# Narrow relation one-hots, two loads moved to ScalarE, and a check moved on GpSimd, in a one-core graph network kernel

## The reference

```
h = relu(layernorm(x))
for W_r, W_sl, W_el in two layers:
    msg = (rel_embed[edge_type] + h[src]) @ W_r
    agg = segment_sum(msg, dst)
    h = rrelu(agg * norm + where(in_degree == 0, h @ W_el, h @ W_sl))
x = x + h
# then one layer of graph attention over the same edges, and x + its output
```

## Time and profile before

| | |
|---|---|
| time, median of 3 runs | 776.05 us (775.11 to 777.04) |
| time of the profiled execution | 776.97 us |
| its span | 775.2 us |
| PE busy | 718.0 us (93%) |
| PE weight loads busy | 534.4 us (69%) |
| DVE busy | 513.9 us (66%) |
| ACT busy | 432.8 us (56%) |
| POOL busy | 279.3 us (36%) |

### The profile page before, as it was taken

The page is one execution under the profiler, slowest core; times in us unless marked ns, Lnnn a source line. Parts: engine busy times, 40 slices in busy tenths (PEclk is TensorE's granted clock), DMA queues, the critical chain, the costliest instruction groups (busy, mean ns, idle before and its releaser), DMA issues.

```text
span 775.2 us, 15480 instructions
## 1 busy us (share of the span) xinstructions
PE 718.0 (93%) x5805; PEld 534.4 (69%) x5805; DVE 513.9 (66%) x906; ACT 432.8 (56%) x1096; POOL 279.3 (36%) x293
## 2 busy tenths in 40 slices
PE   4686789999999999999999999799999999999996
PEld 2565788999899999889889998244444444444456
DVE  5999999988888877333234334245675757576676
ACT  1577566666666666641211223377676767767663
POOL 7299200000001222100000000366675757666664
PEclk9999999999999999999999999799999999999998
DMA  4101000133300000102231112110000100000010
GB/s 132 50 24 45 18 2 9 50 105 65 106 24 8 9 8 9 67 20 81 85 99 39 36 35 61 63 30 0 4 24 1 27 1 14 13 15 13 2 26 21
DMA packets 39763, 27.89 MB, mean 36 GB/s; under 512 B 5311, under 2 KB 38288, under 8 KB 39686
## 3 DMA queue, kind: packets, MB, share of 16 engines
q1 hardware_dynamic: 38514, 25.89, 11.5%
q10 hardware_dynamic: 1172, 0.98, 0.4%
HBM read 13.28 MB, written 10.80 MB: 31 GB/s over the span
## 4 chain that ended last, share of the span: by engine, by line
PE 71%; DMA 8%; DVE 8%; issue 5%; ACT 5%; SPq 2%; ACTq 1%; POOL 1%; POOLq 0%; DVEq 0%
PE sums L1568 17%; PE sums L1551 16%; PE sums L1047 12%; PE sums L1122 9%; PE sums L1086 8%; DVE work L876 3%; DMA x_after_messages<-work 2%; DMA h_attention<-work 2%; DMA work<-in_x 2%; SPq L580 2%; PE sums L1054 1%; DMA counts<-in_x 1%; DVE work L870 1%; ACT counts L1335 1%; PE sums L1061 1%
## 5 line engine op out<-in xcount | busy, mean ns | idle before, releaser
L1647 POOL TENSOR_TENSOR counts<-counts,work 125x500 f32<-125x500 f32 x150 | 165.0, 1100 | 100.0 <-DVE work L1717 94.7
L1717 DVE SCALAR_TENSOR_TENSOR work<-sums,counts 125x500 f32<-125x500 f32 x150 | 101.5, 677 | 106.1 <-ACT sums L1671 100.7
L1086 PE MATMUL sums<-work 125*128 125x196 f16 (+15 forms) x1220 | 153.7, 253 | 17.9 <-DVE work L876 17.9
L1568 PE MATMUL sums<-work 125*128 125x500 f32 (+1 forms) x350 | 159.7, 546 | 6.8 <-DVE work L1717 6.2
L1551 PE MATMUL sums<-work 128*125 128x500 f32 x300 | 152.2, 589 | 0.0
L1666 ACT ACTIVATE sums<-sums,steady 125x500 f32<-125x500 f32 (+1 forms) x157 | 102.0, 650 | 75.0 <-PE sums L1551 71.8
L1335 ACT CAST counts<-sums 128x364 f32 (+38 forms) x305 | 131.6, 473 | 2.3 <-issue 1.1
L870 DVE TENSOR_TENSOR work<-work,counts 125x3024 f16<-125x3024 f16 (+1 forms) x60 | 114.4, 1906 | 25.9 <-PE sums L1088 25.3
L1088 PE MATMUL sums<-work 125*128 125x10 f16 (+15 forms) x800 | 131.5, 194 | 0.0
L876 DVE TENSOR_TENSOR work<-work,counts 125x4200 f16<-125x4200 f16 (+15 forms) x120 | 126.6, 1093 | 0.0
L1047 PE MATMUL sums<-counts 125*128 125x250 f16 (+1 forms) x975 | 119.6, 266 | 3.7 <-ACT work L1263 3.5
(11 more groups left out here) (184 smaller groups left out, 734.8 us busy)
## 6 DMA issues: line engine op xcount, KB each, us to landing
first_columns<-counts SPq DMA_DIRECT2D x5, 610.4 KB
counts<-first_columns SPq DMA_DIRECT2D x5, 610.4 KB
counts<-counts SPq DMA_DIRECT2D x5, 468.8 KB
counts<-in_x SPq DMA_DIRECT2D x5, 312.5 KB
h_nodes<-counts SPq DMA_DIRECT2D x5, 312.5 KB
work<-in_x SPq DMA_DIRECT2D x12, 125.0 KB
x_after_messages<-work SPq DMA_DIRECT2D x12, 125.0 KB
h_attention<-work SPq DMA_DIRECT2D x12, 125.0 KB
```

What stands on the lines that cost most here:

```text
L1086: pe.matmul(win[:, 0:c, cols], lo[:, k * 2 * LO:k * 2 * LO + 128], m[:, k, h0 * w:(h0 + c) * w].rearrange("p (h d) -> p h d", d=w), start= ...
L1568: last = pe.matmul(ps_o[c % 2][:, 0:cols(u) // n], h3[:, source(c, j + i), :], pbuf[u % PB][:, i * NP:i * NP + cols(u) // n], start=j + i ...
L1647: pool.tensor_tensor(a, a, p, ALU.add).then_inc(acc_done, 1)
L1717: dve.scalar_tensor_tensor(pbuf[u % PB], ps_s[u % 4][0:NP, 0:WIDE], float(np.exp(-CLIP)), counts[0:NP, source(c, j), target(c) * WIDE:(tar ...
```

## The change

Relations' one-hots get 100 columns and lie behind all the sources' one-hots of a batch, so that L870 becomes two instructions; the weight load of the relations takes exactly these 100 columns, and the matmul writes 100 partitions. ScalarE issues the loads of the last two pieces of x, after its first small copy. GpSimd waits for `words_done` ahead of its check and no longer behind it.

```diff
-    lo = view(work, at, NP, tiles * 2 * LO + 2, F16)
-    at += tiles * 2 * LO * 2
+    lo = view(work, at, NP, tiles * (LO + RL) + 2, F16)
+    at += tiles * (LO + RL) * 2
...
-            for i in range(5):
+            for i in range(3):
                 sp.dma_start(xs[:, 5 * i:5 * i + 5, :], ...).then_inc(x_in, 16)
...
-            pool.wait_ge(edges_in[0], 16)
+            pool.wait_ge(words_done, 1)
             pool.tensor_copy(final, dst_i[:, EDGES - 1:]).then_inc(outside_set, 1)
             pool.tensor_tensor(steps_i[:, 1:], dst_i[:, :-1], dst_i[:, 1:], ALU.subtract).then_inc(outside_set, 1)
...
             link(pool.memset(most[:, RT + 5:], 0.0))
-
-            pool.wait_ge(words_done, 1)
             pool.wait_ge(outside_set, 5)
...
-                dve.tensor_tensor(lo[:, 0:t * 2 * LO].rearrange("p (t c two) -> p t c two", c=LO // 2, two=2),
-                                  iota_h[:, None, 0:LO].rearrange("p o (c two) -> p o c two", two=2).broadcast_to([NP, 2 * t, LO // 2, 2]),
-                                  key_lo.rearrange("p t (k two) -> p (t k) two", two=2)[:, :, None, :].broadcast_to([NP, 2 * t, LO // 2, 2]), ALU.is_equal)
+                for k, c0, c in ((0, 0, LO), (1, t * LO, RL)):
+                    dve.tensor_tensor(lo[:, c0:c0 + t * c].rearrange("p (t c two) -> p t c two", c=c // 2, two=2),
+                                      iota_h[:, None, 0:c].rearrange("p o (c two) -> p o c two", two=2).broadcast_to([NP, t, c // 2, 2]),
+                                      key_lo[:, :, None, 2 * k:2 * k + 2].broadcast_to([NP, t, c // 2, 2]), ALU.is_equal)
...
-                            pe.matmul(win[:, 0:c, cols], lo[:, k * 2 * LO:k * 2 * LO + 128],
+                            pe.matmul(win[:, 0:c, cols], lo[:, k * LO:k * LO + 128],
                                       m[:, k, h0 * w:(h0 + c) * w]..., start=t == 0, stop=False, skip_group_check=True)
-                        last = pe.matmul(win[:, c:, cols], lo[:, (2 * k + 1) * LO:(2 * k + 1) * LO + 128],
+                        last = pe.matmul(win[0:RL, c:, cols], lo[:, n * GT * LO + k * RL:n * GT * LO + (k + 1) * RL],
                                          r[:, k, :]..., start=False, stop=False, skip_group_check=True)
...
             act.copy(woken, zeros[0:1, 0:1]).then_inc(first_keys, 1)
+            for i in range(3, 5):
+                act.dma_start(xs[:, 5 * i:5 * i + 5, :], ...).then_inc(x_in, 16)
```

More of the change, by code:

```diff
@@ L1230, in _ @@
             act.copy(woken, zeros[0:1, 0:1]).then_inc(first_keys, 1)
+            for i in range(3, 5):
+                act.dma_start(xs[:, 5 * i:5 * i + 5, :], x.rearrange("(j p) f -> p j f", p=NP)[:, 5 * i:5 * i + 5, :]).then_inc(x_in, 16)
             for i, k in enumerate(KEY_ORDER):
```

## The result

The changed kernel takes 772.76 us (median of 12 runs, 769.87 to 773.69), the kernel before beside it on the same chip 775.0 (12 runs). The ratio is 0.9967, with a 95% interval from 0.9955 to 0.998: 2.6 us faster by the ratio, 2.2 us by the medians. The same kernel, measured again on another chip, gave 0.9961 [0.9946, 0.9976], 3.0 us. The forecast was 773.8, or 2.25 us faster than 776.05. The difference is what was met. The time itself, 772.76, lies at what the rival "x early" gave (772.8), but x wasn't early: the kernel before took 1.05 us less beside the changed one than in the three runs on which the forecast was built. The profiled execution took 773.57 us (span 771.8), 3.4 us less than that of before.

The account below looks back on a forecast made before the run. VectorE bounds the path to 115.69 us, but for four places, then PE through the counting. One-hots -2.3, weight loads 0, PE's stretch at 91 us +0.1, head 0 give -2.2 us: 776.05 to 773.8 us, range 771.8 to 778.3.

Parts of the forecast that it names:

- x early: Rival at the head: x lands early, giving 1.1 us more, 3.3 in all, 772.8 us; chance 0.15.
- VectorE's saving: One-hots at L870: 0.147 us saved per four-group batch where VectorE is on the path, 2.3 us in all.
- nothing for batches 8 and 9: One-hots of batches 8 and 9: no gain, since VectorE then waits for the store of h_nodes.
- The narrow load: Relations' weight load at L1088: 100 columns take 46 ns, hidden behind the matmul ahead, cost 0.
- The rival with 9 us: L1088's loads, 130 to 322 us: 86 ns each, not hidden, 9 us cost, 782.8 us; narrow load bare, chance 0.17.
- a price per load: L1088: if a narrow load costs 57 ns whatever its width, 0.8 us is bare in the tiles of w = 10 and 11.
- The head: Loads of x and GpSimd's check, ahead of the statistics: gain 0, covered by the wait for x.
- 2.0 was the step: Batch 0's L870 or L876: collision with GpSimd's moved check costs VectorE 2.0 us, between 1.3 and 2.64.
- the mark of 12.74: ACT's first key copy: later than 12.74 us would show the forecast wrong.
- the signs of a bare load: PE from 130 to 322 us: a stretch over 1 us longer than 192 us would show the forecast wrong.
- Savings swallowed: Rival: store of h_nodes, PE's stretches and ACT's chain leave 0.9 us gain or less, 775.2 us; chance 0.18.
- What lies behind 322 us: Code after the counting: starts earlier by as much as was gained, since none of it waits for anything outside.

Follow-up runs that it names:

- e2: The kernel before with the last two x pieces loaded from ACT, nothing else changed; 776.45 us, ratio 1.0016.
- e3: The kernel before with GpSimd's check moved behind words_done, nothing else changed; 775.82 us, ratio 1.0004.
- e5: The kernel before with only the relations' weight loads narrowed to 100 columns, one-hots still 126 wide; 775.47 us, ratio 1.0005.
- r_e4: The changed kernel with the relations' weights loaded as 128 columns again, repeated on another chip; 772.38 us, ratio 0.9961.
- e1: The kernel before with the one-hots and narrow loads alone, x and GpSimd's check as before; 773.09 us, ratio 0.9978.
- e6: The changed kernel with all five x pieces on SP again; 772.64 us, ratio 0.9971.
- group 2's chip: The chip on which e4, e5, e8 and e10 were timed beside the kernel before.
- group 3's: The chip on which r_e4, e3, e11 and the repeated changed kernel were timed beside the kernel before.
- e7: The changed kernel with all x on SP, each piece issued as two, of 112 and 13 partitions; 772.48 us, ratio 0.9958.
- the wide load's first run, e4: The changed kernel with the relations' weights loaded as 128 columns again, first measurement; 775.83 us, ratio 1.0001.
- e8: The changed kernel with x on SP in pieces of 112 and 13 partitions and GpSimd's selects ahead of its statistics wait; 769.14 us, ratio 0.993.
- e10: The kernel before with L870 cut in two, each still 126 columns wide; 777.05 us, ratio 1.0019.
- e11: The changed kernel with only GpSimd's twelve selects moved ahead of its wait for the statistics; 772.74 us, ratio 0.9972.

## Why the prediction was right

**VectorE's saving (2.3 us): right in size, and in place for the most part.** A pair and its successor lie 2.02 us apart, against 2.17. From batch 2 to 7 the chain gained 0.75 us, which is 5 intervals of 0.15; by the cut without fewer columns it lost 0.35, 5 times the 0.07 of an instruction as such, as worked out.

Behind batch 7 the sum is right and its terms aren't. In the profiled pair batches 7 to 10 lost 0.38 us, where nothing was forecast; 10 to 12 gained 1.14 (two batches: 0.29), 12 to 15 gained 0.88 (three batches: 0.44), 15 to 16 lost 0.57 (0.1 was forecast), and 16 to 25 gained 0.85 (0.53). The first three are explained by GpSimd's last work in this stretch, which prepares the relations' embedding. While it runs, some of VectorE's instructions take longer. Before, one of its rows and two of the slow ones:

```profile
70.42 1.26 POOL L742 TENSOR_TENSOR work<-work 100x256 f32<-100x256 f32 x1
```

```profile
72.29 2.45 DVE L870 TENSOR_TENSOR work<-work,counts 125x4032 f16<-125x4032 f16 x1
74.66 2.20 DVE L876 TENSOR_TENSOR work<-work,counts 125x2400 f16<-125x2400 f16 x2
```

And after, where the same L876 takes 1.56 us and the slow ones are the L869 at 61.87 us (2.74 instead of 2.10, shown above) and others up to 69 us:

```profile
62.29 1.48 POOL L740 TENSOR_TENSOR work<-work 100x256 f32<-100x256 f32 x1
```

Added up over batches 2 to 16, VectorE's records are longer than the shortest of the same line and shape by 1.9 us before and 2.0 after. So the change doesn't save this cost; it moves it, from 70 to 80 us (batches 11 to 13) to 62 to 69 us (10 and 11), because the selects are done sooner and all that GpSimd does behind them comes 7.7 us earlier. Between batches 7 and 10 lie 1.3 us of it after and none before, between 10 and 12 0.65 against 1.5, between 12 and 15 none against 0.44. No step had this. What is left over the forecast up to batch 15 is 0.8 us, and it comes from the step that was mis-sized: nothing for batches 8 and 9, because VectorE waits for the store of h_nodes and a faster VectorE only waits longer. In the profile after, that wait of 0.59 us is nearly gone (L897 starts at 61.12, 0.12 behind the end of L875), since VectorE came late by x and the store took 5.11 instead of 6.13 us. So these two batches gave their 0.29 and the wait some 0.5. This part is luck: e2 and e3, which have L870 in one, don't wait there either.

**The narrow load (0): right**, and the reason holds: it hides behind the matmul ahead. The rival with 9 us is out, and so is a price per load: e5 and r_e4 leave room for 0.2 us, the spread of PE's stretch from 190.73 to 190.89.

**The head.** L811 fell to 0.16 us and batch 0's pair grew by 2.46 - 0.67 = 1.8 us; 2.0 was the step. VectorE was ready for the statistics at 28.42 - 3.03 = 25.39 us, where 26.1 was forecast: besides the pair, the words ahead of batch 0 ended 1.54 us earlier, where 1.1 was forecast. ACT's issues were held up for 7.46 us, hidden as forecast. Its first key copy came at 12.77, 0.03 behind the mark of 12.74, since it waited for PE until then (9.84 us against 9.81). x: the split did not help, and whether it harms stays open. It came at 28.42 us in the profile after, 1.16 late, but at 27.08 in e2, beside 27.13 and 26.78 on SP in e1 and e6; on group 2's chip at 28.85 split and 28.81 and 29.28 on SP; on group 3's at 28.34 to 29.10 split and 26.90 on SP. The 0 stands as the likeliest, and a loss of some 1 us is not excluded. That the queue isn't the limit is shown by e7; few engines per piece fits it.

**Signs.** PE waited 1.4 us in three waits for VectorE from 91 to 130 us, against 3.0 in five, and the chain goes to PE 1.54 us earlier (114.15, where 113.5 was forecast). L897 came at 61.12 us, where 60.7 was forecast, and not behind the store. Batch 2's L869 began at 35.31 us instead of 34.1, late by x. PE's stretch didn't grow, so none of the signs of a bare load appeared.

**The rivals.** x early: no run of the split with whole pieces had it. Savings swallowed: no, but a starved select does just that, in a place that no rival named: it takes back 3.4 us, all of the gain. It is shown in the two profiles that have it. That it also set the median of the wide load's first run (1.0001, its 12 runs from 772.4 to 778.2 us, the repeated one 0.9961) fits, but isn't shown, since only one execution of a group has a profile.

**What lies behind 322 us** was to start earlier by as much and does, but its length isn't constant: from counting's end to the end 453.1 us before, 451.4 after, 450.8 when repeated, 448.5 in r_e4, 453.4 in e3. The 1.6 us of the profiled pair beyond the counting lie within this spread. That they are the change's isn't shown, and the times speak against it: ratios of 0.9961 to 0.9978 are 1.7 to 3.0 us in all, and the counting alone is worth 2.7. One thing that varies is the clock. Window 480 to 510 us of the changed kernel:

```profile
480.00:510.00 30.00, 24.35 (x50) 10.02 (x49) 9.98 (x21) 15.34 (x27) 12.60 (x15) 0.83 0.19 65
```

Of r_e4:

```profile
480.00:510.00 30.00, 23.87 (x59) 10.21 (x59) 11.82 (x24) 17.93 (x32) 15.11 (x17) 1.00 0.21 68
```

PE's granted clock is at the lower of its two levels (1.2 GHz) for 10.2 us there in before, after and e2, and for none of it in r_e4: 59 matmuls against 50 in the same window. Since before and after have the same 10.2 us, this doesn't explain the 1.6 us between them; their cause stays open.

## What to carry to other kernels

When an instruction of a full engine is cut and narrowed, price the columns and the instruction as such apart, from two shapes of the same line; that gave 2.3 us against 2.7 measured, with 0.15 us per batch right where nothing else interferes. Then ask who else wants that engine's port, since the change moves when the two meet: a tiny GpSimd operation on which a third engine waits is better done ahead of VectorE's row of one-hots than among it. And before a 3 us effect is believed of one edit, read where the profile loses it: here the wide load was blamed for a select on another engine.

## What the runs showed of the hardware that was not expected

- Twelve GpSimd instructions of 2 columns beside back-to-back one-hot instructions of VectorE took 11.51, 12.81 or 18.96 us; beside batch 1 and the statistics, 5.52. In two of the twelve profiles that have them among the batches, one of them alone took 16.66 us: the same kernel had 30.08 us in all and 11.51. In e2 and e3 it was one of GpSimd's casts for the relations, 30.9 us from 79 us on; in eight profiles (e4 to e8, e10, e11 and r_e4) a tensor_scalar of 2 columns, at 90 to 97 us, 16.3 to 18.1 us, where before has 1.76. What makes one starve isn't settled.
- GpSimd's work for the relations costs VectorE 1.9 to 2.0 us in ten of the fourteen profiles, whether it lies beside batches 6 to 8 (e8), 10 and 11 (after) or 11 to 13 (before). It costs 1.3 in e2 and e3, and nothing in e4 and e7: in e4 VectorE waits 5.57 us for PE just then, and each of the three subtractions takes 0.64 instead of 1.48 us.
- x's pieces of 125 partitions move at 100 GB/s, of 112 and 13 partitions at 174 to 176.
- The record of the granted clock can miss the head. The prediction wondered at 1.00 beside matmuls at 1.2 GHz pace. Of the kernel before no value ahead of 95.9 us is recorded; e1, e4, e6, e8 and e10, where it is, show 0.50 from about 8 us to between 76 and 87 us. In the window 10 to 20 us of e8:

```profile
10.00:20.00 10.00, 5.96 (x50) 5.64 (x51) 9.47 (x17) 0.95 (x4) 6.54 (x14) 0.50 0.76 176
```

- When PE's clock goes from 1.2 to 2.4 GHz sets its stretch behind batch 15: to batch 16 it is 6.23 us in the profile after, where the granted clock of 88 to 96 us is 0.51, and 4.5 in r_e4, where it is 0.94. From 80 to 88 us PE had been busy for 5.77 and 5.64 us; why the one rose earlier stays open.
